# Order of the K, V and r weights' use in a fused FFN, attention, FFN kernel on eight cores

## What is computed

```python
x = x + 0.5 * ffn(layernorm(x))
x = x + attn(layernorm(x))      # 16 heads of 64
x = x + 0.5 * ffn(layernorm(x)) # the same weights as above

def ffn(x):                     # x_prev: x of the token before, zero at the first
    xr = mu_r * x + (1.0 - mu_r) * x_prev
    xk = mu_k * x + (1.0 - mu_k) * x_prev
    r = sigmoid(xr @ W_r.T)
    k = square(relu(xk @ W_k.T))
    return r * (k @ W_v.T)
```

## Time and profile before

| | us |
|---|---|
| median of the 2 timed runs | 4464.24 |
| the runs | 4427.23, 4501.25 |
| the profiled execution | 4449.14 |
| its span on the slowest core (core 2) | 4447.1 |
| spans of the other cores | 4388.9 to 4432.5 |

### The profile page before, as it was taken

How to read it: one execution, slowest core, us unless ns; L and a number is a source line. 1 busy time by engine, 2 the same in 40 slices (tenths; PEclk the granted TensorE clock), 3 DMA queues, 4 the chain that set the end, 5 groups by cost and what they waited for, 6 DMA issues and landing times.

```text
span 4447.1 us, 71188 instructions; the slowest of 8 cores (4388.9 to 4447.1 us)
## 1 busy us (share of the span) xinstructions
PE 3459.0 (78%) x27248; PEld 2329.0 (52%) x27248; DVE 1472.2 (33%) x2937; ACT 1066.5 (24%) x2297; POOL 286.9 (6%) x412
## 2 busy tenths in 40 slices
PE   0037899996775799998776789999667789999767
PEld 0025555654554664665554555565555565465556
DVE  3412313334323132333423332333423222333441
ACT  2321211223322212222222221222322312222231
POOL 2311000001101000000111100000111100000010
PEclk6567776656897997665788898665688889665679
DMA  7651111001112111000012010100112120100001
GB/s 230 206 192 39 76 39 40 2 2 39 39 58 98 77 47 52 19 2 39 39 58 98 39 76 39 40 2 2 63 53 82 41 109 39 39 2 2 39 39 58
DMA packets 48767, 250.65 MB, mean 56 GB/s; under 512 B 12593, under 2 KB 28977, under 8 KB 43314
## 3 DMA queue, kind: packets, MB, share of 16 engines
q0 software_dynamic: 14720, 197.14, 11.4%
q1 hardware_dynamic: 33714, 48.96, 3.9%
HBM read 208.33 MB, written 37.75 MB: 55 GB/s over the span
## 4 chain that ended last, share of the span: by engine, by line
PE 66%; DVE 12%; DMA 10%; ACT 6%; issue 5%; POOL 1%; DVEq 0%; ACTq 0%; SPq 0%; POOLq 0%
PE gp L528 22%; PE sb L528 12%; PE sb L671 7%; PE pv L766 6%; PE misc L734 4%; PE sb L668 3%; PE sb L605 2%; DMA wsl<-sc_wfv 2%; PE misc L406 2%; PE gp L605 2%; DMA y<-X 2%; DVE bfBl L430 2%; PE misc L439 2%; ACT bfBh L428 2%; PE bca L751 1%
## 5 line engine op out<-in xcount | busy, mean ns | idle before, releaser
L528 PE MATMUL gp<-bfAh,wsl 128*128 128x280 bf16 (+2 forms) x4096 | 697.3, 279 | 216.6 <-DMA wsl<-sc_wfr 127.1
L528 PE MATMUL sb<-bfAh,wsl 128*128 128x280 bf16 x2560 | 485.4, 292 | 85.4 <-DMA wsl<-sc_wfv 56.6
L528 PEld LDWEIGHTS gp<-bfAh,wsl 128*128 128x128 bf16 x4096 | 386.2, 102 | 313.6 <-issue 234.7
L528 PE MATMUL gp<-bfAl,wsl 128*128 128x280 bf16 (+2 forms) x2048 | 547.7, 279 | 0.7 <-issue 0.7
L528 PE MATMUL sb<-bfAl,wsl 128*128 128x280 bf16 x1280 | 373.2, 292 | 0.0
L528 PEld LDWEIGHTS sb<-bfAh,wsl 128*128 128x128 bf16 x2560 | 255.5, 101 | 158.5 <-issue 96.1
L668 PE MATMUL sb<-msb,idt 128*128 128x128 bf16 x832 | 230.7, 277 | 94.5 <-DVE qbl L640 62.7
L734 PE MATMUL misc<-eh,ones 128*1 128x128 bf16 (+2 forms) x832 | 192.8, 257 | 117.0 <-DVE rb L755 88.1
L691 DVE TENSOR_TENSOR el<-e,eh 128x384 bf16<-128x384 f32 (+1 forms) x160 | 80.8, 505 | 592.2 <-ACT eh L688 592.2
L528 PE MATMUL gp<-bfBh,wsl 128*128 128x280 bf16 x1024 | 196.5, 294 | 59.0 <-ACT katmp L554 59.0
L528 PE MATMUL gp<-aeh,wsl 128*128 128x128 bf16 (+1 forms) x2560 | 232.9, 231 | 12.0 <-DVE ael L787 11.1
(11 more groups left out here) (176 smaller groups left out, 6035.3 us busy)
## 6 DMA issues: line engine op xcount, KB each, us to landing
wsl<-sc_wfr POOLq DMA_DIRECT2D x8, 4096.0 KB, 14.9
wsl<-sc_wfk POOLq DMA_DIRECT2D x8, 4096.0 KB, 17.3
wsl<-sc_wfv POOLq DMA_DIRECT2D x8, 4096.0 KB, 13.0
wsl<-sc_wak POOLq DMA_DIRECT2D x4, 4096.0 KB, 14.1
wsl<-sc_wav POOLq DMA_DIRECT2D x4, 4096.0 KB, 14.1
wsl<-sc_wq POOLq DMA_DIRECT2D x4, 4096.0 KB, 13.4
wsl<-sc_wo POOLq DMA_DIRECT2D x4, 4096.0 KB, 13.9
X<-x SPq DMA_DIRECT2D x8, 1120.0 KB, 5.8
```

The costliest lines, as they stand in the source:

```text
L528: ins = t.matmul(out_ap, wap(slot, reg, ci, d0, dn), rhs, start=first, stop=(ci == NCH - 1 and j == 2))
```

## The change

Three edits in the main loop. First, `attn_V_tile(wav_u, 2, at)` is issued ahead of `attn_K_half(wak_u, 1, at)` and not behind it. Second, the load of wfr for f2 is no longer a group in the background work of the weave. Third, it is issued after that weave instead, directly ahead of the load of wfk. The slots stay the same.

```diff
@@ -886,8 +886,8 @@
             weave(capture(lnmix, 1, at + " ln2", True),
                   groups_of(attn_K_half, wak_u, 0, at)
                   + groups_of(attn_V_tile, wav_u, 0, at) + groups_of(attn_V_tile, wav_u, 1, at))
+            attn_V_tile(wav_u, 2, at)
             attn_K_half(wak_u, 1, at)
-            attn_V_tile(wav_u, 2, at)
             qslot, qsres = load_use("wq")
             attn_Q_pair(qslot, qsres, 0, 2, at)
             weave_even(capture(attn_pairs, q, 0, 0, qslot, qsres, at),
@@ -906,12 +906,11 @@
             attn_wo(q, 2, oslot, osres, at)
             bgb = (groups_of(attn_pairs, q, 3, 128, qslot, qsres, at)
                    + groups_of(attn_Q_pair, qslot, qsres, 4, 1, at)
-                   + [capture(load_use, "wfr")]
                    + groups_of(attn_pairs, q, 4, 0, qslot, qsres, at,
                                preempt=lambda: attn_wo(q, 3, oslot, osres, at))
                    + groups_of(attn_wo, q, 4, oslot, osres, at))
             weave(capture(cm_ln3), bgb, lead=12)
-            wr = (wsl[1], ["wsl1_hi", "wsl1_lo"])
+            wr = load_use("wfr")
             wk = load_use("wfk")
             weave(capture(lnmix, 1, f2),
                   groups_of(ffn_proj_half, wr, 0, "r", f2) + groups_of(ffn_proj_half, wk, 0, "k", f2))
```

## The result

The changed kernel is slower by 1.1%: the ratio to the kernel before is 1.0109, with a 95% interval of 1.0082 to 1.0135. The forecast was 1.0115. The median of all its 15 runs is 4491.5 us, against 4421.1 us for 14 of the kernel before. The profiled execution took 4460.4 us.

A forecast was written before the change was run, and what follows sets the result against it. The prediction took TensorE's in-order queue plus its stops for weight loads as the bound. Its sum was 4449.1 + 48.5 + 3 + 0 = 4500.6, say 4500 us, with a range of 4465 to 4545.

The forecast's parts named there:

- Step 1: Before the Q projection, the V tile no longer covers the wq load, so PE waits idle: +48.5 us, -6/+6.
- Step 2: Q projection runs at a lower granted clock after the longer wq wait: +3 us, between 0 and +6.
- Step 3: In f2, wfr loaded after the weave stays just hidden before the first r matmul: 0 us, bounds -4 to +11.
- Rival A: wfr lands late in f2: small form 4511 us, chance 0.08; large form, whole load shows, 4560 us, chance 0.03.
- B: Granted clock of a whole stage (f1, K, V) falls to about 0.8: 4547 us, +2.2%, chance 0.06.
- C: Longer stop frees the clock, pass 0's dense stretch at about 0.8 vanishes: 43 us less, 4457 us, chance 0.04.

The follow-up runs named there:

- e2: Kernel before with only V tile 2 moved ahead of K half 1, wfr loaded inside the weave as before: ratio 1.0103.
- e1: Changed kernel with V tile 2 back behind K half 1, so only the later wfr load is left: ratio 1.0041 (0.9992 to 1.0089).
- e3: Changed kernel with half of V tile 2 (26 matmuls) put back behind K half 1: ratio 1.0125 (1.0040 to 1.0209).
- e8: Second timing of e3, half of V tile 2 behind K half 1: ratio 1.0094 to the kernel before, fastest run 4433.5 us.
- e9: Kernel before with 5 of 8 k-projection groups of half 1 moved between last r and first v matmul, f1 and f2: ratio 0.9791, fastest 4310.1 us.
- e10: Kernel of e9 with V tile 2 moved ahead of K half 1: fastest run 4366.3 us, no usable ratio.
- e12: Kernel of e9 with the later wfr load, V tile still behind K half 1: ratio 0.9820 to the kernel before, fastest 4317.3 us.
- e5: Changed kernel with the wfr load issued behind the wfk load on POOL's queue: ratio 1.0318 to the kernel before, fastest 4564.8 us.
- e11: Kernel of e9 with the first half of V tile 3 moved behind V tile 2: ratio 0.9795 to the kernel before, fastest 4308.8 us.
- e4: Changed kernel with 48 unused matmuls between K half 1 and the first Q matmul: ratio 1.0118 to the kernel before.

## Why the prediction was right

**Step 1, the V tile as cover (+48.5 us): confirmed.** The wait for wq rose by 47.4 us, e2 shows the cost with the swap alone (ratio 1.0103), e1 shows no clear change without it, and e3 and e8 gain back about half with half the tile. The bound of 6 us either way was enough.

**Step 2, the clock after the long wait (+3 us): about right on the slowest core, too large in the mean.** On core 6, the slowest of the changed kernel, the Q projection of pass 0 took 21.13 us before, at 1.00, and 24.00 after; in the later passes it took 22.8 before, behind a short wait and at 0.79, and 22.5 to 22.8 after. In all that is 2.4 us. On core 5, where the short wait of the kernel before had already lowered the clock in pass 0, it is 1.1 us less than before; the mean is under 1 us, leaving out cores 2 and 3, whose clock was already lower before, from 410 us on. I had charged 0.4 us to each later pass from the wfv rows, whose 0.69 was the lower end. The granted clock after the waits of passes 1 and 2 was 0.78 and 0.82 for 8 us, the level of the earlier trace rows behind the short wait. The term is small because the clock was already down before the change, and not because a long wait costs no clock: e9 and e10 show some 1.6 us a place. The windows of the changed kernel (PE busy first, PEclk third from the end):

```profile
611.80:619.80 8.00, 8.00 (x48) 6.07 (x49) 0.48 (x1) 0.47 (x1) 0.00 (x0) 0.63 0.00 0
1662.00:1670.00 8.00, 7.96 (x58) 6.45 (x59) 0.60 (x2) 0.95 (x2) 0.00 (x0) 0.78 0.00 0
2714.00:2722.00 8.00, 8.00 (x61) 6.59 (x62) 0.96 (x2) 0.95 (x2) 0.00 (x0) 0.82 0.01 2
```

**Step 3, the later wfr load (0 us): right within a few us.** The margin forecast for pass 0 was 0.6 us, found was 1.4 us; for pass 3 it was 3.1 and 3.1, though the load took 14.6 us there and not 12.5, since PE came later as well. That every margin held owes something to luck: the smallest of the 32 was 0.25 us, and e1 has one of 16.0 us that was missed by 0.99. By e1 and e12 it costs 2 to 7 us, inside the bound of -4 to +11. Rival A did not come true, though e5 shows that its large form was real, and dearer than I priced it: 104 us and not 60, since both loads then run at once.

The moved reciprocals changed which row waits and not how long. They come with the later wfr load: e1 has these waits like the changed kernel, e2 like the kernel before. PE's waits for the copy to rb, changed kernel first, kernel before second:

```profile
PE bca L751 <- DVE rb L755: 59.3, 4, 15.3
```
```profile
PE misc L734 <- DVE rb L755: 88.1, 26, 16.5
```

On one and the same core (core 6) the entry of line 734 fell from 88.0 to 25.7 us while that of line 751 came up from nothing to 59.3, so 85.0 in place of 88.0, and the wait for mb_sb (line 454), which the reciprocals now precede on DVE, rose from 6.2 to 9.1 us. The two cancel, as the prediction had it.

**The base.** The relative forecast is better than the absolute one. I added 51 us to an execution of 4449.1 us whose slowest core had 0.79 in pass 0's dense stage from 410 to 470 (core 3 had 0.81, the other six 0.91 or more). The usual time of the kernel before is 4405 to 4415, and the changed kernel's is 4455 to 4462, so 4500 us is 40 us too high. That it lies near the median of all 15 runs, 4491.5, is luck; the 50 us are not.

**Rivals B and C** concern this clock. In the changed kernel's profile both dies are at 0.755 and the window from 420 to 480 has 0.91 at core 6, as six of the eight cores of the kernel before had it. So nothing here speaks for B. What C forecast, no such stretch at 0.8, is what this trace has, and the two profiled executions are only 11 us apart; the distance of 34 to 44 us between the profiled execution of before and the usual times matches the 43 us that I had for that stretch. But nothing ties it to the change: the kernel before takes its usual 4405 to 4415 us without any edit, and in one run of the changed kernel (4491.5 us) the four cores of one die still have a mean clock of 0.747 against 0.755.

## What to carry to other kernels

When two buffers take turns, look at what TensorE does between the last reader of the old content and the first reader of the new one: independent work in that gap is worth its own time up to the length of the load, and little or nothing beyond (e11). Moving such work a step earlier leaves every instruction and every load as it was and still costs its whole duration. Then look for the same gap elsewhere: here it stood open in eight other places, and filling them was worth twice what the change lost.

## What was not expected of the hardware

Filling a 14 us wait with matmuls that nothing uses changed the time by some 2 us at most (4458.5 against the usual 4460; e4). That does not make a long stop free of a cost in clock: a wait of 3 to 4 us was left there, with 0.79 behind it. Against a wait of about 2 us with the clock at 1.00, a stop of 13 to 15 us costs more than itself: 192 matmuls took 22.8 in place of 21.1 us behind it (e10, e9), and the first 48 took 8.46 in place of 5.88 us behind one for wfv (before, e9). A short wait does not always keep the clock: waits of 1.5 to 2 us for wq stand ahead of 0.79 in the kernel before and ahead of 1.00 in e9; what decides is not shown.

Two 4 MB loads issued 0.55 us apart landed after 17.0 and 26.3 us, against 12.4 to 15.0 us for the single wfr loads of f2 in the changed kernel; PE wanted the second one first and waited 27.7 us (e5). And those single loads differ by that much from core to core within one execution; the waits of the cores for weights differ by some 20 us (295.6 us for weights in all on core 0 of the changed kernel, 317.0 on core 6).
